# An attention loop over 16 batches on one Trainium2 core: the order of its steps is rewritten over the border between two batches

## The chip, the cores and the metric

The kernel runs on one core of a Trainium2 chip. The metric is device time in microseconds (us) of one execution. Three runs of the kernel before gave 2103.26, 2096.0 and 2092.29 us, median 2096.0. The execution that the profiler recorded took 2089.78 us, with a span of 2088.0 us from its first to its last instruction.

## The reference

The input x has 16 batches of 512 tokens of width 256, all float32. The output is x plus attention plus a mixture of experts, both computed on the layer-normed x:

```python
xn = _layernorm(x)
q, k, v = xn @ Wq.T, xn @ Wk.T, xn @ Wv.T          # 16 heads of 16
q, k = _rope(q, k)
scores = where(causal, -inf, q k^T / 4); attn = softmax(scores) v
logits = xn @ router_w.T + router_bias              # 32 experts, top 4
h = silu(xn @ gate_w.T) * (xn @ up_w.T)             # per expert, width 128
out = sum over the top 4 of score * (h @ down_w.T)  # routed part
out += silu(xn @ sgate_w.T) * (xn @ sup_w.T) @ sdown_w.T   # shared part, width 512
x = x + attn @ Wo.T + out
```

## The kernel before

The kernel has three phases, one after the other, with a barrier between them. Phase A does, batch by batch, the layer norm, the projections, attention, the shared expert and the routing; it scatters the normed tokens into per-expert regions in DRAM (`values`, `table`) and stores x + attention + shared expert (`sum_dram`). Phase B runs 288 blocks of 128 tokens through their experts. Phase D gathers and adds. The change touches phase A alone.

Phase A is written as a list of steps, `ORDER`. Each engine has a handler for the steps in which it takes part, and every engine walks through the same list, so the list is at once the program order of TensorE (PE), VectorE (DVE), ScalarE (ACT), GpSimd (POOL) and of SyncE's DMA queue (SP). Engines meet only by semaphores. An instruction that waits holds up everything behind it on its engine. `FIRST_STEPS` prepares batch 0; then `ORDER` runs for batches 0 to 14, and each body also prepares the next batch (layer norm, q, k, v, routing: the steps in `NEXT_STEPS`); the last batch runs without those and with loads of the expert weights put in (`last_steps`).

The steps, with their lines in the profile of before:

- `("gate", m)`, `("up", m)` (PE L915, two matmuls each), `("gth", m)` (DVE L694) and the product (DVE L702, in the step `up`): the shared expert's hidden layer, m = 0 to 3. The tanh is ACT L570.
- `("s1", g, u)`: six steps for each of four head groups g. PE (L931, L935) computes scores of four heads, DVE (L715) takes the row maxima. `("negsplit", g)` (DVE L726, L727), `("negT", g)` (PE L945, ACT L588) and a small DMA (SP L411) bring the negated maxima into rows of `q_st`.
- `("s2", g, u)`: five steps per group. PE (L962, L973) computes transposed scores less the maxima, ACT (L600) the exponentials. `("av", g, kt)` (PE L990) multiplies with v; `("avT", g)` (DVE L736 to L749) transposes and divides.
- `("down", t)` (PE L1002) and `("oproj", p)` (PE L1011): the shared expert's second matmul and the output projection, summed in one PSUM tile; DVE L757 adds x, SP L417 stores.
- Next batch: `lnA` (DVE L646 to L651, after the load of x by SP L397), `lnB` (L655 to L663), `lnC` (L670); `xT` (PE L880, ACT L526) transposes into `xn_t`; `("qk", j)` (PE L896, DVE L682 to L685 for the rotary embedding, POOL L481, `part0` on ACT L546, POOL L485) makes two-part q and k in `parts`; `("vr", t)` (PE L905, ACT L537, L538) makes v and router logits; `("stack", c)` is 12 SP DMAs (L391) of 128 KB from `parts` to `q_st` and `k_st`, c = 0 for head groups 0 and 1, c = 1 for groups 2 and 3. `route` (DVE L765 to L787), `exps` (ACT L605), `rank` (PE), `rankA`, `rankB`, `rankC` (DVE) pick experts and slots; `copy` (ACT L578) and `("scat", t)` (POOL L494, L496, eight indirect DMAs each) write tokens out.

PSUM buffers set a second order. The steps s1 and s2 share two tiles, `ps_u`, strictly in turn: a step waits until the s1 or s2 step two before it has been read, by DVE for s1 and by ACT for s2. Most other PE steps share three tiles, `ps_g`, in turn. `plans` works out, from the list, whose reader each step waits for.

Of the kernel before, what the change touches and what calls it, by code (L numbers as in the profile page):

```python
# [68 lines left out]
def hold(eng, passed):  # L69
# [9 lines left out]
    ("rankC",), ("gate", 0), ("placeV",), ("s1", 0, 0), ("gth", 0), ("up", 0), ("s1", 0, 1), ("copy",), ("s1", 0, 2),  # L79
    ("gate", 1), ("s1", 0, 3), ("s1", 0, 4), ("gth", 1), ("scat", 0), ("up", 1), ("lnA",), ("gate", 2), ("s1", 0, 5),  # L80
    ("negsplit", 0), ("gth", 2), ("scat", 1), ("s1", 1, 0), ("up", 2), ("s1", 1, 1), ("negT", 0), ("gate", 3),
# [11 lines left out]
    ("exps",), ("stack", 1), ("down", 0), ("down", 1), ("rankA",), ("av", 3, 0), ("av", 3, 1), ("av", 3, 2),  # L93
    ("av", 3, 3), ("avT", 3), ("rankB",), ("down", 2), ("down", 3), ("oproj", 0), ("oproj", 1),
# [3 lines left out]
def attention_steps(with_next):  # L98
    return [s for s in ORDER if with_next or s[0] not in NEXT_STEPS]


def last_steps(order):


    s, piece = [], 0
    for step in order:
        s.append(step)
        if step == ("rankC",):
            s.append(("fill_rows",))
        if step == ("scat", NT - 1):  # L110
            s.append(("fill",))
# [13 lines left out]
     ("stack", 0), ("stack", 1), ("loaded", 1), ("route",), ("exps",),  # L125
     ("rank",), ("rankA",), ("rankB",)]
# [3 lines left out]
            "vr": ("logits",), "tables": ("cos_t", "sin_t"), "rank": ("ranked",)}  # L130
NEXT_STEPS = ("lnA", "lnB", "lnC", "xT", "tables", "qk", "vr", "part0", "stack", "route", "exps", "rank", "rankA",
              "rankB")
# [5 lines left out]
def plans(steps, last_banks, last_units):  # L138


    banks, units, last_banks, last_units = {}, {}, list(last_banks), list(last_units)
    nb = nu = 0
    for step in steps:
        idx, ahead = step[1] if len(step) > 1 else 0, int(step[0] in NEXT_STEPS)
        for k, name in enumerate(BANKS_OF.get(step[0], ())):
            banks[step, k] = (nb, last_banks[nb])
            last_banks[nb] = (name, idx, ahead)
            nb = (nb + 1) % len(last_banks)
        if step[0] in ("s1", "s2") or step == ("down", 0):
# [44 lines left out]
def phase_a(nc, sb_, sem, ident, identb, iota_e, counts, we_gu, we_d, ps_g, ps_u, ps_av, x, wqkvr, wgu_e, wd_e, wo, wgu_s, wd_s, bias,  # L194
            rope_cos, rope_sin, values, sum_dram, table):
    stack = ExitStack()
    with stack:
# [50 lines left out]
        xn_t = in_gu([P, KC, SEQ])  # L248
# [58 lines left out]
        we_in, fill_chain, fill_ready, filled = sem("we_in"), sem("fill_chain"), sem("fill_ready"), sem("filled")  # L307
        neg_parts, tanh_done, av_out, exps, chosen_ready = \
# [14 lines left out]
        body = attention_steps(True)  # L323
        tail = last_steps(attention_steps(False))
# [36 lines left out]
        def _(sp):  # L361
# [32 lines left out]
            def x_load(nb):  # L394
# [19 lines left out]
            def store(b, step, env):  # L414
                if step[1] == 1:
                    sp.wait_ge(S["sums"], 2 * b + 2)
                    sp.dma_start(tokens(sum_dram, b), osum[:, :, :]).then_inc(sum_out, 16)  # L417
# [8 lines left out]
            run(sp, {"loaded": loaded, "stack": stack_rows, "gate": gate, "negT": neg_store, "oproj": store})  # L426
# [92 lines left out]
        def _(act):  # L519
            def xT(nb, step, env):  # L520
                t, bank = step[1], env[0][step, 0][0]
                act.wait_ge(pe["xT"], NT * nb + t + 1)
                if t == 0 and not env[3]:

                    act.wait_ge(pe["up"], NM * nb)
                nc.scalar.activation(xn_t[:, :, t * P:(t + 1) * P],  # L526
# [64 lines left out]
            def s2(b, step, env):  # L591
# [5 lines left out]
                if u == 0:  # L597

                    act.wait_ge(pe["av"], NG * b + (g - 1 if g >= 2 else 0))
# [38 lines left out]
        def _(dve):  # L638
            front = Chain(dve, dve_front, 2 + 3 + 3 * 3 + 6 + 7, passed_dve)
            back = Chain(dve, dve_chain, NG + NG + 4, passed_dve)  # L640
# [78 lines left out]
            def negsplit(b, step, env):  # L719
# [6 lines left out]
                back.link(b, nc.vector.tensor_copy(np_[:, :, 0, :], n_))  # L726
# [3 lines left out]
            def avT(b, step, env):  # L730
# [8 lines left out]
                back.link(b, nc.vector.reciprocal(rden[:], rows[:, :, DH]))  # L739
# [11 lines left out]
            def oproj(b, step, env):  # L751
# [703 lines left out]
```

## Time and profile before

| | before |
|---|---|
| runs, us | 2103.26, 2096.0, 2092.29 |
| profiled execution / its span, us | 2089.78 / 2088.0 |
| PE, DVE busy | 86%, 66% |
| ACT, POOL busy | 36%, 48% |
| phase A ends (last store to `sum_dram` issued) | 1435.9 us after the start |

Busy shares are averages over three unlike phases. PE is TensorE's matmul row; its ends are modelled. A row of the timeline gives start, duration, engine, line, operation, `out<-in`, how many instructions are merged, and in brackets the idle time before and what ended it. In names of tiles `we_gu` and `we_d` stand for buffers of phase A that share the memory of the expert weights (x, xn, xn_t, parts among them).

### The profile page before, as it was taken

How to read it: one execution, taken by the hardware profiler on the slowest of the kernel's cores; microseconds unless marked ns; L12 is line 12 of the kernel's file. 1: busy time of each engine (PE TensorE's matmuls, PEld its weight loads, DVE VectorE, ACT ScalarE, POOL GpSimd, SP SyncE). 2: the span in 40 equal slices, each digit the busy share in tenths (PEclk: the TensorE clock that was granted, in tenths of full speed). 3: DMA queues.
4: the chain of work that ended last, by engine and by line, in shares of the span. 5: the costliest groups of instructions: out<-in, count | busy, mean ns of one | idle time of the engine just before them, and what ended most of it. 6: DMA issues, size and time to landing. Idle time of an engine off the chain costs nothing. (4 is left out here: it accounts for less than half of the span.)

```text
span 2088.0 us, 41196 instructions
## 1 busy us (share of the span) xinstructions
PE 1800.1 (86%) x10415; PEld 1092.9 (52%) x10416; DVE 1377.0 (66%) x3411; ACT 758.2 (36%) x1667; POOL 998.2 (48%) x993
## 2 busy tenths in 40 slices
PE   5898999999999999999999999995999999999300
PEld 2354554545545455454554545543888888888300
DVE  6667668667686675866767667651566666666487
ACT  2334333342343423334234342331444444444200
POOL 5455445553454534545345453473555555555200
PEclk8999999999999999999999999976999999999755
DMA  6251541624506246052460624565555555556499
GB/s 136 78 123 37 108 93 39 127 50 87 111 26 121 54 84 111 27 124 45 90 111 29 121 49 86 104 185 197 150 167 170 168 178 167 172 170 181 136 352 326
DMA packets 217741, 255.29 MB, mean 122 GB/s; under 512 B 74421, under 2 KB 166334, under 8 KB 217536
## 3 DMA queue, kind: packets, MB, share of 16 engines
q1 hardware_dynamic: 160000, 161.90, 33.8%
q0 software_dynamic: 35840, 71.63, 10.7%
q10 hardware_dynamic: 21824, 20.98, 3.1%
q14 instruction: 59, 0.48, 0.1%
q8 instruction: 18, 0.29, 0.1%
HBM read 112.54 MB, written 94.64 MB: 99 GB/s over the span
## 5 line engine op out<-in xcount | busy, mean ns | idle before, releaser
L715 DVE TENSOR_REDUCE neg<-ps_u 128x2 f32<-128x768 f32 (+3 forms) x384 | 391.5, 1044 | 149.7 <-PE ps_u L935 145.4
L494 POOL DMA_INDIRECT table<-entry,slot x256 | 254.4, 994 | 360.6 <-ACT xs L578 260.0
L1204 POOL DMA_INDIRECT y_dram<-yb,ent x288 | 283.4, 984 | 223.5 <-issue 169.7
L496 POOL DMA_INDIRECT values<-xs,slot x256 | 248.6, 971 | 83.3 <-issue 83.3
L915 PE MATMUL ps_g<-we_gu 128*128 128x512 f32 x512 | 243.6, 609 | 0.0
L600 ACT ACTIVATE probs<-ps_u 128x1024 f32<-128x1024 f32 x160 | 159.3, 1021 | 160.0 <-PE ps_u L973 159.6
L600 ACT ACTIVATE we_d<-ps_u 128x1024 f32<-128x1024 f32 x160 | 161.1, 1022 | 152.5 <-PE ps_u L973 152.3
L962 PE MATMUL ps_u<-q_st,k_st 50*128 50x512 f32 (+3 forms) x1024 | 171.6, 394 | 50.7 <-DMA q_st<-neg_t 14.7
L931 PE MATMUL ps_u<-k_st,q_st 48*128 48x128 f32 (+3 forms) x1024 | 185.6, 400 | 31.1 <-DVE neg L715 20.7
L481 POOL TENSOR_TENSOR we_d<-we_d 128x512 f32<-128x512 f32 x64 | 81.3, 1271 | 211.4 <-DVE we_d L685 208.6
L931 PEld LDWEIGHTS ps_u<-k_st,q_st 48*128 48x128 f32 x1024 | 88.2, 189 | 168.2 <-issue 74.2
L1255 PE MATMUL ps_u<-we_d,h_t 128*128 x576 | 173.7, 383 | 0.0
L570 ACT ACTIVATE we_gu<-ps_g 128x512 f32<-128x512 f32 x64 | 38.2, 597 | 349.1 <-PE ps_g L915 349.1
L1336 DVE TENSOR_SCALAR wh<-ent 128x1 f32<-128x1 f32 x288 | 44.3, 154 | 174.2 <-ACT tnh L1151 130.1
L962 PEld LDWEIGHTS ps_u<-q_st,k_st 50*128 50x128 f32 x1024 | 89.0, 201 | 132.6 <-ACT probs L600 38.1
L1241 PE MATMUL ps_g<-we_gu,x_t 128*128 x576 | 150.1, 383 | 3.7 <-issue 3.7
L1241 PE MATMUL ps_av<-we_gu,x_t 128*128 x576 | 149.7, 383 | 1.6 <-issue 1.6
L915 PEld LDWEIGHTS ps_g<-we_gu 128*128 128x128 f32 x512 | 92.8, 194 | 80.0 <-issue 75.5
L1329 DVE COPY x_t<-ps_g 128x256 f32<-128x256 f32 x288 | 120.6, 419 | 12.9 <-PE ps_g L1230 10.9
L1002 PE MATMUL ps_u<-w_d,hid 128*128 128x256 f32 x512 | 125.9, 402 | 0.6
L935 PE MATMUL ps_u<-mask_qk,identb 128*128 128x128 bf16 (+1 forms) x768 | 125.5, 246 | 0.0
L1165 ACT ACTIVATE yb<-ps_u 128x256 f32<-128x256 f32 x288 | 110.6, 384 | 31.2 <-PE ps_u L1255 5.1
(157 smaller groups left out, 3012.7 us busy)
## 6 DMA issues: line engine op xcount, KB each, us to landing
xg<-values SPq DMA_DIRECT2D x288, 128.0 KB
ys<-y_dram SPq DMA_DIRECT2D x64, 512.0 KB, 5.5
q_st<-we_gu SPq DMA_DIRECT2D x192, 128.0 KB, 7.7
k_st<-we_gu SPq DMA_DIRECT2D x192, 128.0 KB, 9.5
we_gu<-x SPq DMA_DIRECT2D x16, 512.0 KB, 6.0
xres<-x SPq DMA_DIRECT2D x16, 512.0 KB, 5.4
sum_dram<-osum SPq DMA_DIRECT2D x16, 512.0 KB, 4.7
we_gu<-wgu_e ACTq DMA_DIRECT2D x16, 512.0 KB, 5.0
```

The source lines that it names most:

```text
L494: pool.indirect_dma_start(table[:, :], bass.IndirectOffsetOnAxis(ap=slot[:, k:k + 1], axis=0), entry[:, k, :], None).then_inc(scattered, 16)
L496: pool.indirect_dma_start(values[:, :], bass.IndirectOffsetOnAxis(ap=slot[:, k:k + 1], axis=0), xs[:, k // TOPK, :], None).then_inc(scatte ...
L600: nc.scalar.activation(probs[g % 2][:, u, :], ps_u[env[1][step][0]][:, :, :].rearrange("p a n -> p (a n)"), ACT.Exp, scale=SCALE).then_inc ...
L715: nc.vector.tensor_reduce(neg[:, g % 2, i, :, k0:k0 + nk], ps[:, :, 0:nk * n].rearrange("p a (k n) -> p a k n", n=n), AX.X, ALU.max, negat ...
L915: ins = nc.tensor.matmul(ps[:, :], w_gu[:, c, lo:lo + P], xn_t[:, c, :], start=(c == 0), stop=(c == KC - 1))
L931: nc.tensor.matmul(ps[:, a, k * n:(k + 1) * n], q_st[rows, h, i * P:(i + 1) * P], k_st[rows, h, 0:n], start=(k == 0), stop=False, skip_gro ...
L935: ins = nc.tensor.matmul(dst, identb[:], mask_qk[:].rearrange("p (o n) -> p o n", o=1).broadcast_to([P, nk, P]), start=False, stop=True, s ...
L962: nc.tensor.matmul(ps[:, a, lo:lo + n], k_st[rows, h, kt * P:(kt + 1) * P], q_st[rows, h, kt * P:SEQ], start=(lo == 0), stop=False, skip_g ...
L1002: nc.tensor.matmul(ps[:, t // 2, (t % 2) * D:(t % 2 + 1) * D], hid[:, m, t * P:(t + 1) * P], w_d[:, m, :], start=(t % 2 == 0 and m == 0), ...
L1204: pool.indirect_dma_start(y_dram[:, :], bass.IndirectOffsetOnAxis(ap=ent[k][:, 0:1], axis=0), yb[k][:, :], None, bounds_check=TOKENS * TOP ...
L1241: ins = nc.tensor.matmul(ps_gu[s][:, 0:2 * HE], x_t[s][:, c * P:(c + 1) * P], w_gu[:, bass.ds(e, 1), c, :], start=(c == 0), stop=(c == KC ...
L1255: nc.tensor.matmul(ps_y[s][:, 0:D], h_t[s][:], w_d[:, bass.ds(e, 1), :], start=True, stop=True).then_inc(y_ps, 1)
```

## The change

The list is written anew, and some steps belong to another batch than the body they stand in. A function `ahead_of` says which: s1, negsplit and negT of group 0 now belong to the next batch (+1) and stand at the end of the body; av and avT of group 3 and the output sum belong to the batch before (-1) and stand at its start. The body has four parts, one for each group; in each, the s1 steps of one group alternate with the s2 steps of the group before it, and av of the group before that stands behind the first s1 step.

```diff
 ORDER = [
+    ("rankC",), ("xload",), ("copy",), ("scat", 0), ("s1", 1, 0),
+    ("av", 3, 0), ("av", 3, 1), ("av", 3, 2), ("av", 3, 3), ("s1", 1, 1), ("avT", 3), ("gate", 0), ("placeV",), ("scat", 1),
+    ("s1", 1, 2), ("gth", 0), ("out", 0, 0), ("s2", 0, 0), ("s1", 1, 3), ("lnA",), ("s2", 0, 1), ("out", 0, 1),
+    ("s1", 1, 4), ("lnB",), ("s2", 0, 2), ("scat", 2), ("out", 1, 0), ("s1", 1, 5), ("s2", 0, 3), ("negsplit", 1),
+    ("lnC",), ("out", 1, 1), ("s2", 0, 4), ("negT", 1), ("store",), ("xres",),
+
+    ("s1", 2, 0), ("av", 0, 0), ("av", 0, 1), ("av", 0, 2), ("av", 0, 3), ("s1", 2, 1), ("avT", 0),
+    ("xT", 0), ("xT", 1), ("xT", 2), ("xT", 3), ("up", 0), ("s1", 2, 2), ("gate", 1), ("s2", 1, 0), ("s1", 2, 3), ("gth", 1),
+    ("s2", 1, 1), ("qk", 0), ("s1", 2, 4), ("s2", 1, 2), ("up", 1), ("s1", 2, 5), ("part0", 0), ("s2", 1, 3),
+    ("negsplit", 2), ("qk", 1), ("s2", 1, 4), ("negT", 2),
+
+    ("s1", 3, 0), ("av", 1, 0), ("av", 1, 1), ("av", 1, 2), ("av", 1, 3), ("s1", 3, 1), ("part0", 1), ("avT", 1),
+    ("stack", 0), ("scat", 3), ("vr", 0), ("s1", 3, 2), ("gate", 2), ("s2", 2, 0), ("s1", 3, 3), ("gth", 2), ("s2", 2, 1),
+    ("up", 2), ("s1", 3, 4), ("s2", 2, 2), ("qk", 2), ("s1", 3, 5), ("s2", 2, 3), ("negsplit", 3), ("vr", 1),
+    ("s2", 2, 4), ("negT", 3), ("part0", 2),
+
+    ("s1", 0, 0), ("av", 2, 0), ("av", 2, 1), ("av", 2, 2), ("av", 2, 3), ("s1", 0, 1), ("vr", 2), ("vr", 3), ("avT", 2),
+    ("s1", 0, 2), ("gate", 3), ("s2", 3, 0), ("s1", 0, 3), ("route",), ("gth", 3), ("s2", 3, 1), ("up", 3), ("s1", 0, 4),
+    ("s2", 3, 2), ("qk", 3), ("s1", 0, 5), ("s2", 3, 3), ("exps",), ("negsplit", 0), ("rank",), ("part0", 3), ("s2", 3, 4),
+    ("rankA",), ("negT", 0), ("rankB",), ("stack", 1),
 ]
+def ahead_of(step):
+    if step[0] in NEXT_STEPS or (step[0] in ("s1", "negsplit", "negT") and step[1] == 0):
+        return 1
+    if step[0] in ("out", "store") or (step[0] in ("av", "avT") and step[1] == NG - 1):
+        return -1
+    return 0
```

`FIRST_STEPS` gets the s1 steps, negsplit and negT of group 0 of batch 0 ahead of `route`. The first body leaves out the steps with -1; a separate `LAST_ORDER` serves the last batch, and an `EPILOGUE` does its av, avT, output sum and store. The loop now takes two batches per turn, since the transposed input has two buffers:

```diff
-        xn_t = in_gu([P, KC, SEQ])
+        xn_ts = [in_gu([P, KC, SEQ]) for _ in range(2)]
...
-            with eng.Fori(1, BATCH - 1) as b:
-                assert (lb, lu) == tuple(map(one_later, steps(body, b, b + 1, False, lb, lu)))
-            steps(tail, BATCH - 1, None, False, lb, lu)
+            with eng.Fori(0, (BATCH - 2) // 2) as i:
+                lb1, lu1 = steps(ORDER, 2 * i + 1, 1, False, lb, lu)
+                assert (lb1, lu1) == (lb, lu), (lb, lb1, lu, lu1)
+                assert (lb, lu) == steps(ORDER, 2 * i + 2, 0, False, lb, lu)
+            lb, lu = steps(tail, BATCH - 1, 1, False, lb, lu)
+            steps(EPILOGUE, BATCH, 0, False, lb, lu)
...
-                    act.wait_ge(pe["up"], NM * nb)
+                    act.wait_ge(pe["up"], NM * (nb - 1))
```

`down` and `oproj` become `out`: for each 128 tokens the four matmuls with `w_d` and the two with `w_o` stand together, in a tile of `ps_g` where they had one of `ps_u`:

```diff
+            def out_part(b, step, env):
+                p_, half = step[1:]
+                t = 2 * p_ + half
+                if half == 0:
+                    bank_of(step, 0, env)
+                ps = ps_g[env[0][("out", p_, 0), 0][0]][:, half * D:(half + 1) * D]
+                if t == 0:
+                    pe_.wait_ge(S["hidden"], done("hidden", b, NM - 1))
+                for m in range(NM):
+                    nc.tensor.matmul(ps, hid[:, m, t * P:(t + 1) * P], w_d[:, m, :], start=(half == 0 and m == 0),
+                                     stop=False, skip_group_check=True)
+                if t == 0:
+                    pe_.wait_ge(S["attn_t"], done("attn_t", b, KC - 1))
+                for c in range(KC):
+                    ins = nc.tensor.matmul(ps, attn_t[:, c, t * P:(t + 1) * P], w_o[:, c, :], start=False,
+                                           stop=(c == KC - 1), skip_group_check=True)
+                if half == 1:
+                    ins.then_inc(pe["sum"], 1)
```

The load of x for the next batch is a step of its own (`xload`), as are `xres` and `store`. In the last batch the loads of the expert weights are issued later, beside s2 of groups 2 and 3 instead of beside nearly all s2 steps:

```diff
-        if step[0] == "s2" and step[1:] != (0, 0) and piece < GU_PIECES:
-            s.append(("load_gu", piece))
-            piece += 1
+        if step[0] == "s2" and step[1] >= 2:
+            n = 2 if piece < 12 else 1
+            s += [("load_gu", piece + k) for k in range(n)]
+            piece += n
```

Two semaphores (`neg_high`, `rden_ready`) replace links of the chain semaphore in negsplit and avT; they order the same instructions.

## Rows read from the trace of the kernel before

**Rows 1.** The page: busy time and share of the span of each engine.

```profile
PE 1800.1 (86%) x10415; PEld 1092.9 (52%) x10416; DVE 1377.0 (66%) x3411; ACT 758.2 (36%) x1667; POOL 998.2 (48%) x993
```

**Rows 2.** Timeline of SyncE's queue: stores of batches 0, 1 and 14, a stack, an x load.

```profile
139.36 0.39 SPq L417 DMA_DIRECT2D sum_dram<-osum  x1
224.67 0.42 SPq L417 DMA_DIRECT2D sum_dram<-osum  x1
632.99 3.80 SPq L391 DMA_DIRECT2D q_st<-we_gu  x6
654.47 0.41 SPq L397 DMA_DIRECT2D we_gu<-x  x1
1347.63 0.42 SPq L417 DMA_DIRECT2D sum_dram<-osum  x1
```

**Rows 3.** Waits of PE, 139.4 to 225 us: total us, times, longest; first of seven.

```profile
PE ps_g L945 <- DVE neg_p L727: 1.1, 1, 1.1
```

**Rows 4.** Timeline of PE in one body.

```profile
578.30 0.50 PE L931 MATMUL ps_u<-k_st,q_st 48*128 48x512 f32 x2
...
578.95 0.44 PE L931 MATMUL ps_u<-k_st,q_st 48*128 48x128 f32 x4
...
585.86 0.50 PE L962 MATMUL ps_u<-q_st,k_st 50*128 50x512 f32 x2
...
587.69 0.51 PE L962 MATMUL ps_u<-q_st,k_st 50*128 50x384 f32 x4 [0.46 <-ACT we_d L600]
...
617.04 2.36 PE L990 MATMUL ps_av<-probs,v_pad 128*32 128x512 f32 x32
...
630.45 0.40 PE L945 MATMUL ps_g<-ident_r,neg_p 128*8 128x128 f32 x4 [1.07 <-DVE neg_p L727]
...
634.26 0.50 PE L962 MATMUL ps_u<-q_st,k_st 50*128 50x512 f32 x2 [1.12 <-DMA q_st<-neg_t]
...
644.89 3.72 PE L1002 MATMUL ps_u<-w_d,hid 128*128 128x256 f32 x16
648.45 3.62 PE L1011 MATMUL ps_u<-w_o,attn_t 128*128 128x256 f32 x16
651.90 1.88 PE L915 MATMUL ps_g<-we_gu 128*128 128x512 f32 x4
```

**Rows 5.** Timeline of DVE: lnA's first, a maximum, a rotary step's last, route's first, avT.

```profile
577.59 1.40 DVE L646 BATCH_NORM_STATS2 stats<-we_gu 128x6 f32<-128x256 f32 x4
...
579.86 1.23 DVE L715 TENSOR_REDUCE neg<-ps_u 128x2 f32<-128x1024 f32 x1
...
596.66 0.69 DVE L685 TENSOR_TENSOR we_d<-ps_g,we_gu 64x512 f32<-64x512 f32 x1
...
630.23 0.29 DVE L765 TENSOR_TENSOR lg<-logits,bias_bc 128x128 f32<-128x128 f32 x1
...
634.61 0.72 DVE L736 STREAM_TRANSPOSE av<-ps_av 128x512 f32<-128x512 f32 x1
```

**Rows 6.** Timeline of POOL: the second POOL instruction behind that rotary step.

```profile
599.75 1.27 POOL L485 TENSOR_TENSOR we_gu<-we_d,we_gu 128x512 fp32r<-128x512 f32 x1 [0.89 <-ACT we_gu L546]
```

**Rows 7.** DMAs issued at 647.5 to 648.6, then 654.3 to 655 us: KB, us to landing.

```profile
k_st<-we_gu SPq DMA_DIRECT2D x2, 128.0 KB, 11.3
...
we_gu<-x SPq DMA_DIRECT2D x1, 512.0 KB, 8.5
```

**Rows 8.** Timeline of DVE, then of PE, in the first body.

```profile
62.59 1.41 DVE L646 BATCH_NORM_STATS2 stats<-we_gu 128x6 f32<-128x256 f32 x4 [8.18 <-DMA we_gu<-x]
...
66.05 0.80 PE L931 MATMUL ps_u<-k_st,q_st 48*128 48x256 f32 x4 [7.88 <-DVE neg L715]
```

**Rows 9.** Stretches: busy us of PE, PEld, DVE, ACT, POOL; clock, DMA share, GB/s.

```profile
61.00:71.00 10.00, 4.95 (x14) 2.65 (x15) 7.85 (x24) 0.59 (x1) 7.76 (x8) 0.52 0.14 45
...
1430.00:1435.00 5.00, 5.00 (x24) 4.21 (x23) 1.04 (x2) 0.00 (x0) 3.42 (x4) 1.00 1.07 388
```

**Rows 10.** Timeline of ACT's queue: the first weight load, in the last batch.

```profile
1368.23 0.46 ACTq L618 DMA_DIRECT2D we_gu<-wgu_e  x1
```

More of the change, by code:

```diff
@@ L78, with last_steps @@
 ORDER = [
[L79 to L81 removed]
[11 rows of a table removed]
[L93 to L102 removed]
+    ("rankC",), ("xload",), ("copy",), ("scat", 0), ("s1", 1, 0),
[3 rows of a table added]
+    ("lnC",), ("out", 1, 1), ("s2", 0, 4), ("negT", 1), ("store",), ("xres",),
[11 rows of a table added]
+    ("rankA",), ("negT", 0), ("rankB",), ("stack", 1),
+]
+LAST_ORDER = [
+    ("rankC",), ("fill_rows",), ("copy",), ("scat", 0), ("scat", 1), ("scat", 2), ("scat", 3), ("fill",), ("s1", 1, 0),
[3 rows of a table added]
+    ("out", 1, 1), ("s2", 0, 4), ("up", 0), ("negT", 1), ("store",), ("xres",),
[6 rows of a table added]
+    ("negsplit", 3), ("s2", 2, 4), ("negT", 3),
+    ("av", 2, 0), ("av", 2, 1), ("av", 2, 2), ("av", 2, 3), ("avT", 2), ("s2", 3, 0), ("s2", 3, 1), ("s2", 3, 2),
+    ("s2", 3, 3), ("s2", 3, 4),
+]
+EPILOGUE = [
+    ("av", 3, 0), ("av", 3, 1), ("av", 3, 2), ("av", 3, 3), ("avT", 3), ("out", 0, 0), ("out", 0, 1), ("out", 1, 0),
+    ("out", 1, 1), ("store",),
+]
+def last_steps():
     s, piece = [], 0
[L106 removed]
+    for step in LAST_ORDER:
         s.append(step)
[L108 to L111, printed above, removed]
[L112 to L114 removed]
+        if step[0] == "s2" and step[1] >= 2:
+            n = 2 if piece < 12 else 1
+            s += [("load_gu", piece + k) for k in range(n)]
+            piece += n
         if step == ("s2", NG - 1, NU2 - 1):
@@ L124 @@
      ("qk", 2), ("vr", 2), ("part0", 2), ("qk", 3), ("vr", 3), ("part0", 3),
-     ("stack", 0), ("stack", 1), ("loaded", 1), ("route",), ("exps",),
-     ("rank",), ("rankA",), ("rankB",)]
+     ("stack", 0), ("stack", 1), ("loaded", 1)] + [("s1", 0, u) for u in range(NU1)] + \
+    [("negsplit", 0), ("negT", 0), ("route",), ("exps",), ("rank",), ("rankA",), ("rankB",)]
 BANKS_OF = {"gate": ("gated",), "up": ("hidden",), "negT": ("neg_t",), "xT": ("xn_t",), "qk": ("rope",),
@@ L424, in loaded @@
                                  ).then_inc(table_set, 16)
-            run(sp, {"loaded": loaded, "stack": stack_rows, "gate": gate, "negT": neg_store, "oproj": store})
+            run(sp, {"loaded": loaded, "stack": stack_rows, "xload": x_load, "xres": xres_load, "negT": neg_store,
+                     "store": store})
             sp.wait_ge(sum_out, 16 * BATCH)
@@ L738, in avT @@
                 rows = av[:].rearrange("p (b c) -> p b c", c=2 * DH)
-                back.link(b, nc.vector.reciprocal(rden[:], rows[:, :, DH]))
+                nc.vector.reciprocal(rden[:], rows[:, :, DH]).then_inc(rden_ready, 1)
+                dve.wait_ge(rden_ready, NG * b + g + 1)
                 if s == 0:
@@ L749, in avT, with out_sum @@
                     nc.vector.transpose(attn_t[:, c, :], attn[:, c, :]).then_inc(S["attn_t"], 1)
-            def oproj(b, step, env):
-                p_, u = step[1], env[1][("down", 0)][0]
+            def out_sum(b, step, env):
+                p_, half = step[1:]
+                if half == 0:
+                    return
+                bank = env[0][("out", p_, 0), 0][0]
                 dve.wait_ge(pe["sum"], 2 * b + p_ + 1)
@@ L851, in _ @@
             run(dve, {"lnA": ln_a, "lnB": ln_b, "lnC": ln_c, "qk": qkv, "gth": gated, "up": hidden, "s1": s1, "negsplit": negsplit,
-                      "avT": avT, "oproj": oproj, "route": route, "rankA": rank_a, "rankB": rank_b, "rankC": rank_c,
+                      "avT": avT, "out": out_sum, "route": route, "rankA": rank_a, "rankB": rank_b, "rankC": rank_c,
                       "fill_rows": fill_rows, "loaded": loaded})
@@ L1038, in _ @@
                       "gate": hidden_part("gate", 0), "up": hidden_part("up", 1), "s1": s1, "negT": negT, "s2": s2, "av": av_,
-                      "down": down, "oproj": oproj, "rank": rank})
+                      "out": out_part, "rank": rank})
 def phase_bcd(nc, sb_, sem, ident, iota_e, counts, we_gu, we_d, ps_g, ps_u, ps_av, values, sum_dram, table, y_dram,
```

92 lines of the change are left out of this document (39 added, 53 removed), and 20 rows, old and new, of tables (LAST_ORDER, ORDER).

## The prediction, written before the changed kernel was run

> **What bounds the kernel now.** I read the page first, then the stores to `sum_dram` as marks of the batches, then the waits of PE, then the timelines of one body. The page has PE busy for 86% of the span and each other engine that computes for two thirds or less [rows 1]. The stores come 224.67 - 139.36 = 85.3 us apart from batch 0 to 1, and (1347.63 - 139.36) / 14 = 86.3 us apart on average [rows 2]. In the 85.3 us body PE waits in seven ways, 5.4 us in all: 1.1 us for the maxima (negT behind negsplit) [rows 3], 1.1 us for their rows (s2 behind the small DMA), and short waits of 0.2 to 0.5 us for a `ps_u` tile [rows 4]. So a body is 79.9 us of PE work. No order of steps changes that work, and 5.4 us a body, some 80 us over 15 bodies, is nearly all that a better order can win.
>
> **The parts of the change.** The same matmuls, maxima and DMAs run in another order, so the sum is one of waits. A, B, C, D are the four parts of the new body, as the list is broken.
>
> *What goes.* Between negT of a group and its first s2 stand six to nine us of PE work in the new list. The way from the one to the other took 634.26 - 630.85 = 3.4 us [rows 4], so that 1.1 us goes, and so does the one at negT where qk, vr or out stands ahead of it. The second `xn_t` lets xT run before the last up; it costs nothing, the ACT copies are the same ones, and no row shows PE waiting for that buffer, so it brings nothing by itself. An `out` step is half of the two down steps' 3.56 us and a quarter of the 3.45 us of both oproj steps, 2.7 us [rows 4], the same work as before. The two new semaphores stand where links of a chain stood: nothing, either way.
>
> *Short waits for `ps_u`.* An s2 that needs the tile of an earlier s2 can start 587.69 - 585.86 = 1.8 us after that one's start: its matmuls, the exponential and two hand-overs [rows 4]. In each part (s2,0), (s1,3), (s2,1) stand in a row, 1.2 us from the first to the third, so 0.6 us is lost; and av waits for the last exponential behind 1.55 us of negT and s1, 0.25 us. Four parts: 3.4 us. Bounds: 0 (the rows of before show 0.46, not always) and 5.
>
> *Part D, route.* route holds DVE for 634.61 - 630.23 = 4.4 us [rows 5]. Before, it stood behind the last maximum of a group. Now it stands between (s1,0,3) and (s1,0,4). After the maximum of (s1,0,3), DVE does route 4.4, gth and hid 0.65 each (like the 0.69 of rows 5, starts overlapping), then the maximum of (s1,0,4), 1.2: 6.9 us. PE is then 1.0 us ahead and has s2 0.65, up 1.8, s1 0.55, s2 0.75, qk 1.8 and 0.6 of short waits to do, 6.2 us [rows 4], before (s1,0,5) needs that tile: 6.9 + 1.0 - 6.2 = 1.7 us of waiting. Next DVE does the rotary step, three instructions of 0.69 [rows 5], and the maximum of (s1,0,5), 1.2: 3.4 us, while PE has s1, s2 and rank, 1.8 us, before (s2,3,4) needs the tile: 1.6 us. Together 3.3. Bounds: 0, since route stood beside PE work without such a wait before, and 5, if DVE comes 1.7 us late to route.
>
> *Part C.* By the same count avT with its second transpose (2.1 us) and the rotary step ahead of (s1,3,5)'s maximum leave PE waiting 0.9 us at (s2,2,4). The stack of groups 0 and 1 is now needed when D starts. It can go once the parts of qk 1 are made, 601.02 - 597.35 = 3.7 us after the rotary step [rows 5, 6], 4.8 us into C. Of such DMAs 24 ran from 632.99 until about 647.8 + 11.3 = 659.1 [rows 2, 7]: 1.0 each and some 2 to start. Twelve are 14.4 us, so the stack is there 19.2 us into C, whose own length I count as 18.9: 0.3 us. Bounds: 0 and 3.
>
> *Part A, the load of x*, the largest term. Stack 1 is the last SP step of a body, and `xload` follows it in the same queue. Before, the stacks were issued from 632.99, 19 us ahead of the body's end. Now stack 1 waits for qk 3, near the end of D, behind route on DVE: its rotary step is done 2.4 us before D ends, and 3.7 us more go through POOL and ACT; and SP first issues the rows of negT 0. Behind negT a stack went out 632.99 - 630.85 = 2.1 us later [rows 2, 4], and ACT now has one exponential to do first. I take 3.0 us into the next body. The stack ends at 3.0 + 14.4 = 17.4. Behind the stack of before, three transfers of 512 KB landed until 654.47 + 8.5 = 663.0, (663.0 - 659.1) / 3 = 1.3 us each [rows 2, 7], so x lands at 18.7. DVE comes to lnA at 11 us and stands there. Behind lnA (2.2 us) come the first output sum (0.7) and the maximum of (s1,1,4) (1.2) [rows 5], done at 22.8. PE comes to (s1,1,5), which needs that tile, after five s1 (3.0; one is 578.95 - 578.30 = 0.65), av 2.3, gate 1.8, three out 8.1, three s2 2.1 and 0.85 of short waits, at 18.1 us [rows 4]. It waits 4.7 us. The first body shows this chain: DVE stood 8.18 us at L646 for x behind a 2 MB DMA, and PE 7.88 us for the maximum behind it [rows 8]. Bounds: 0 if the stack moves fast, 8 if it goes out 3 us later.
>
> One rule of the Trainium skill speaks for a short stack: "DMA: Bandwidth & Descriptors", section "Anatomy of one DMA", fits a transfer as 2.0 us plus its bytes over 436 GB/s. By that, an estimate, 1.57 MB take 5.6 us, x lands near 10 us, before DVE asks, and the term is nothing; the trace, 26.1 us for twice the bytes [rows 2, 7], disagrees and decides.
>
> *A body.* 3.4 + 3.3 + 0.9 + 0.3 + 4.7 = 12.6 us of waits for the 5.4 of before: 85.3 + 7.2 = 92.5 us, against the mean of 86.3: +6.2, and +87 over fourteen bodies. The clock is left as in the 85.3 us body.
>
> *Ends of the phase.* In the first body the table's DMA holds back x, and now also the rows for s2 of group 0. PE went on at 66.05 [rows 8]; now it can at about 61.5, but gates 1 to 3 and ups 0 to 2 (10.8 us) no longer stand ahead of that wait, and 1.3 us of s1 does: 10.8 - 1.3 - 4.5 = +5. In the last batch the loads of the weights, 12.6 MB, began at 1368.23 [rows 10], 21 us after the store of 14 [rows 2]. Now they begin some 38 us before the last store lands. At the 388 GB/s of rows 9 they take 32 us, at the 280 that most slices of that stretch come to, 45: 0 to 7 us stick out; the transpose in the epilogue, no longer covered by down, costs 1.5. Together +6.
>
> **Forecast.** 2089.8 + 87 + 5 + 6 = 2188 us for an execution like the profiled one. The median of the runs shown, 2096.0, is 0.3% above that one; on its scale, 2194 us.
>
> **Rivals.**
> - *x arrives in time.* The stack moves faster when it is alone; the same engines moved 388 GB/s [rows 9], by which it takes 4 us and 2 to start, and x lands near 10. The 4.7 and the 0.3 go: +1.2 us a body, 2089.8 + 17 + 11 = 2118, or 2124 by the median. For it: that rate. Against it: 1.0 us per DMA held to the end of the stacks, when the scatters were over.
> - *Faster: the waits for the maxima go and DVE keeps up.* The place is D and A: DVE reaches route 1.7 us earlier than I count, and x is there. What remains is the 3.4 us for `ps_u`: 83.3 us, 3.0 under the mean, 2089.8 - 42 + 11 = 2059 (2065 by the median). It decides when a body's waits are under the 5.4 us of before. For it: DVE is busy 66% [rows 1]. Against it: rows 8.
> - *Worse: the clock.* Around the 7.88 us wait the granted clock was 0.52 for 10 us [rows 9], half speed, 1.2 GHz. With two such waits a body (A, D), one or two stretches more of a third of that, 1.7 us lost in each, add 24 to 48 us: 2218 to 2242.
> - *No net change.* Gains and waits cancel, 2086 to 2106.
>
> **Chances.** Forecast 0.50, clock 0.16, x in time 0.15, faster 0.13, no change 0.06. A measurement of this kernel can tell about 0.5% from no change. So: faster 0.14, within 0.06, slower 0.80. The range 2105 to 2235 holds the first two and most of the third; the forecast's own is 2160 to 2215.
>
> **What would show it.** In the trace after: stores some 92 us apart; in every body a DVE wait of 5 to 8 us at L646's place for the DMA of x, and behind it a PE wait of 4 to 5 us in s1; a PE wait of 1 to 3 us for the maxima during route; no wait over 0.5 us at negT or for the rows of maxima. The forecast is wrong if x lands before 11 us into the body, or if DVE needs under 5.6 us from route to the next maximum.

## The result, and the profile after

The changed kernel takes 2193.65 us (median of four runs, 2189.65 to 2196.76) against 2097.03 us before: ratio 1.0446, 95% interval 1.0417 to 1.0474, slower by 97 us. The profiled execution took 2189.65 us, its span is 2187.4, 99.4 us over the span before.

The stores of SyncE's queue mark the batches of the changed kernel, as those of [rows 2] do before (start, duration, queue, line):

```profile
168.53 0.41 SPq L453 DMA_DIRECT2D sum_dram<-osum  x1
...
726.13 0.41 SPq L453 DMA_DIRECT2D sum_dram<-osum  x1
820.72 0.41 SPq L453 DMA_DIRECT2D sum_dram<-osum  x1
...
1467.80 0.40 SPq L453 DMA_DIRECT2D sum_dram<-osum  x1
1537.35 0.40 SPq L453 DMA_DIRECT2D sum_dram<-osum  x1
```

Fourteen periods from the first store take 1299.3 us, 92.8 each; before, 1208.3 us, 86.3 each. That is +91.0 us. The first store comes 29.2 us later than before, because more now stands ahead of it, and the last one follows the fifteenth after 69.5 us instead of 88.3: +10.4 for both ends. Phases B and D are 2 us shorter.

The same 14 bodies by what PE waited for (total us, times, longest), in the changed kernel (in the kernel before, the waits of the 14 bodies come to 70.5 us, 5.0 a body):

```profile
PE ps_u L974 <- DVE neg L752: 65.5, 51, 5.5
PE ps_u L1005 <- DVE neg L752: 37.1, 28, 1.6
PE ps_u L974 <- issue: 16.3, 6, 2.8
PE ps_u L1005 <- ACT probs L637: 14.6, 28, 0.5
PE ps_u L1005 <- ACT we_d L637: 8.5, 15, 0.6
PE ps_av L1033 <- ACT we_d L637: 3.7, 20, 0.2
PE ps_av L1033 <- ACT probs L637: 2.5, 14, 0.2
```

L974 is s1, L1005 is s2, and L752 the row maximum. "issue" is time in which PE waited for nothing that the profile shows. With 0.4 us for the stack these are 148.6 us, 10.6 a body. And the busy time of PE, PEld, DVE, ACT and POOL, the clock, the DMA share and GB/s in the same stretch, after and before:

```profile
168.50:1467.80 1299.30, 1146.40 (x6832) 600.38 (x6828) 850.41 (x1774) 457.86 (x700) 576.93 (x559) 0.94 0.37 75
```
```profile
139.40:1347.60 1208.20, 1131.75 (x6834) 599.54 (x6833) 849.79 (x1793) 450.67 (x700) 583.09 (x560) 0.96 0.39 80
```

PE's busy time grew by 14.7 us, at a clock of 0.94 instead of 0.96; the rest of the 91 us, 76.5, is idle time. PE's number of instructions is the same within two and the busy times of the other engines are the same within 8 us: no work was added.

Body 726.1 to 820.7 shows where. First PE, then DVE (in brackets the wait before, and what ended it):

```profile
762.65 0.50 PE L1005 MATMUL ps_u<-q_st,k_st 50*128 50x256 f32 x4 [1.10 <-DVE neg L752]
...
781.02 0.49 PE L974 MATMUL ps_u<-k_st,q_st 48*128 48x512 f32 x2 [1.63 <-DVE neg L752]
784.32 0.63 PE L1005 MATMUL ps_u<-q_st,k_st 50*128 50x256 f32 x4 [1.58 <-DVE neg L752]
...
810.79 0.79 PE L974 MATMUL ps_u<-k_st,q_st 48*128 48x512 f32 x2 [4.38 <-DVE neg L752]
```
```profile
806.57 1.41 DVE L683 BATCH_NORM_STATS2 stats<-we_gu 128x6 f32<-128x256 f32 x4 [7.12 <-DMA we_gu<-x]
```

and SyncE's queue between them, the rows of negT 0, the twelve DMAs of stack 1, the load of x, and that load's time to landing in the last row (KB, us):

```profile
787.04 1.27 SPq L448 DMA_DIRECT2D q_st<-neg_t  x2
788.49 3.80 SPq L431 DMA_DIRECT2D q_st<-we_gu  x6
792.34 3.80 SPq L431 DMA_DIRECT2D k_st<-we_gu  x6
796.43 0.39 SPq L437 DMA_DIRECT2D we_gu<-x  x1
```
```profile
we_gu<-x SPq DMA_DIRECT2D x1, 512.0 KB, 10.0
```

x lands near 806.4, DVE has been standing at lnA for 7.1 us, and PE for 4.4 us behind it. So far the trace is the forecast's.

The next body is another matter. The loop turns in it, near 883 us. PE, then DVE:

```profile
885.23 0.69 PE L974 MATMUL ps_u<-k_st,q_st 48*128 48x128 f32 x4 [2.76 <-issue]
```
```profile
886.57 0.18 DVE L858 TENSOR_TENSOR entry<-pr,zs 128x16 f32<-128x16 f32 x1 [2.85 <-issue]
...
901.25 1.41 DVE L683 BATCH_NORM_STATS2 stats<-we_gu 128x6 f32<-128x256 f32 x4 [2.61 <-DMA we_gu<-x]
```

PE and DVE each stand 2.8 us, one soon after the other, for nothing that the profile shows; ACT has rows until 884.8. DVE then waits only 2.6 us for x, and PE doesn't wait behind it. (The expectations of e2 and e7 below say that all engines stand there; the rows show it for PE and DVE.) The profile page's row of the instruction queue q8 (packets, MB, share of the DMA engines) says what the turn does, before and after:

```profile
q8 instruction: 18, 0.29, 0.1%
```
```profile
q8 instruction: 83, 1.36, 0.3%
```

Before, no packet of q8 falls between 212 and 1348 us: as I read it, the engines held the code of the loop. After, 57 fall between 250 and 1300 us, 16 KB each, with two some 4 us apart at each turn (882.3 and 886.7 here). The 8 KB packets of a second instruction queue, q14, behave alike: none between 209 and 1368 us before, 30 between 250 and 1300 us after. The loop over two batches has twice the code, and it is fetched again on each turn. The prediction had not seen that.

### The profile page after: what moved, and what is told of

The parts are those of the page before. It is cut to its first block and busy times, and to the rows that moved or that the text cites. A ratio compares the mean times of both kernels' runs of the same rounds, so it can differ in the third digit from the quotient of the medians.

```text
span 2187.4 us, 40804 instructions
## 1 busy us (share of the span) xinstructions
PE 1813.2 (83%) x10415; PEld 1092.0 (50%) x10416; DVE 1379.0 (63%) x3411; ACT 766.6 (35%) x1667; POOL 993.0 (45%) x993
## 5 line engine op out<-in xcount | busy, mean ns | idle before, releaser
L752 DVE TENSOR_REDUCE neg<-ps_u 128x2 f32<-128x768 f32 (+3 forms) x384 | 399.9, 1042 | 290.1 <-PE ps_u L978 284.9
L531 POOL DMA_INDIRECT table<-entry,slot x256 | 249.4, 974 | 184.9 <-issue 106.8
L974 PE MATMUL ps_u<-k_st,q_st 48*128 48x128 f32 (+3 forms) x1024 | 190.1, 410 | 105.9 <-DVE neg L752 74.0
L958 PE MATMUL ps_g<-we_gu 128*128 128x512 f32 x512 | 247.2, 605 | 0.0
L637 ACT ACTIVATE probs<-ps_u 128x1024 f32<-128x1024 f32 x160 | 163.9, 1024 | 198.6 <-PE ps_u L1016 196.9
L1005 PE MATMUL ps_u<-q_st,k_st 50*128 50x512 f32 (+3 forms) x1024 | 169.3, 390 | 74.2 <-DVE neg L752 41.8
L974 PEld LDWEIGHTS ps_u<-k_st,q_st 48*128 48x128 f32 x1024 | 91.2, 196 | 259.0 <-issue 124.5
L1005 PEld LDWEIGHTS ps_u<-q_st,k_st 50*128 50x128 f32 x1024 | 86.8, 198 | 168.2 <-DVE neg L752 76.4
L1048 PE MATMUL ps_g<-w_d,hid 128*128 128x256 f32 x512 | 133.0, 406 | 0.0
L938 PE MATMUL ps_g<-we_gu 128*128 128x512 f32 x256 | 121.4, 597 | 0.0
L522 POOL TENSOR_TENSOR we_gu<-we_d,we_gu 128x512 fp32r<-128x512 f32 x64 | 81.4, 1272 | 83.6 <-ACT we_gu L583 83.6
```

The lines of the kernel that those rows point to most:

```text
L531: pool.indirect_dma_start(table[:, :], bass.IndirectOffsetOnAxis(ap=slot[:, k:k + 1], axis=0), entry[:, k, :], None).then_inc(scattered, 16)
L637: nc.scalar.activation(probs[g % 2][:, u, :], ps_u[env[1][step][0]][:, :, :].rearrange("p a n -> p (a n)"), ACT.Exp, scale=SCALE).then_inc ...
L752: nc.vector.tensor_reduce(neg[:, g % 2, i, :, k0:k0 + nk], ps[:, :, 0:nk * n].rearrange("p a (k n) -> p a k n", n=n), AX.X, ALU.max, negat ...
L958: ins = nc.tensor.matmul(ps[:, :], w_gu[:, c, lo:lo + P], xn_ts[env[4]][:, c, :], start=(c == 0), stop=(c == KC - 1))
L974: nc.tensor.matmul(ps[:, a, k * n:(k + 1) * n], q_st[rows, h, i * P:(i + 1) * P], k_st[rows, h, 0:n], start=(k == 0), stop=False, skip_gro ...
L1005: nc.tensor.matmul(ps[:, a, lo:lo + n], k_st[rows, h, kt * P:(kt + 1) * P], q_st[rows, h, kt * P:SEQ], start=(lo == 0), stop=False, skip_g ...
```

## The experiments

Every kernel was run beside the kernel before. One thing has to be known to read them: on each of the three chips of the later runs the kernel before itself took 2579 to 2631 us in place of 2097 (in the profiled run r1, 469 of 498 us of the excess are there when the last store of phase A is issued). The ratios of the first ten kernels hold under that disturbance alone; the last pair removes most of it.

**The load of x alone** (e1, repeated as e5). It is issued from ScalarE's queue, so that it isn't behind the stack:

```diff
-            run(sp, {"loaded": loaded, "stack": stack_rows, "xload": x_load, "xres": xres_load, "negT": neg_store,
+            run(sp, {"loaded": loaded, "stack": stack_rows, "xres": xres_load, "negT": neg_store,
...
-            run(act, {"loaded": loaded, "xT": xT, "tables": tables, ...
+            run(act, {"xload": x_load, "loaded": loaded, "xT": xT, "tables": tables, ...
```

> The changed kernel with one edit: the load of x is issued by ScalarE's queue instead of SyncE's, so it no longer queues behind the 12 DMAs of stack 1. Theory (the load of x behind stack 1 is what holds DVE at lnA and PE behind it): x lands some 5 us after the body starts, the DVE wait for x (7.1 us in one body of two, 2.6 in the other) and the PE wait of 4.4 us behind it go, seven or eight bodies gain 3 to 4.4 us: 2160 to 2170 us. Rival 1 (the shared DMA engines are what x waits for, whatever the queue): x still lands at about 16 us, time unchanged, 2190 us. Rival 2 (DVE is the bound in that part anyway): the wait for x goes, PE waits as long for the maxima, 2185 to 2195 us.

> The changed kernel, with the load of x issued from ScalarE's queue instead of behind the stacks in SyncE's. In the earlier run of this kernel everything in phase A took some 30% longer than in the first measurements (bodies of 115 to 120 us, before and after alike), and the x wait was too small a share to be read. This run repeats it. If bodies are again near 93 us in the changed kernel's way: the DVE waits for x go from 75.5 us in all to under 15 us, the PE waits behind them (4.4 us in each body without a loop turn, seven of them) go, and the loop turn's 2.8 us gap stays: 2193.7 - 31 = some 2163 us, ratio to the kernel before 1.031. Rival: the gap moves to another wait, and the ratio stays at 1.04 to 1.045. If phase A is slow here too (kernel before over 2500 us): ratio 1.018, as it was, with the DVE wait for x near 4 us.

Ratio to the kernel before 1.0178 (1.0133 to 1.0224), then 1.0203 (1.0163 to 1.0243). DVE's waits for x, over the whole execution, in the changed kernel as first measured, in its repetition r2 under the disturbance, and in e1 (4.1 us in e5):

```profile
DVE stats L683 <- DMA we_gu<-x: 75.5, 15, 8.3
```
```profile
DVE stats L683 <- DMA we_gu<-x: 11.1, 3, 4.9
```
```profile
DVE stats L683 <- DMA we_gu<-x: 4.3, 1, 4.3
```

x lands 3.6 us after its issue in e1 and 7.6 us in the changed kernel (medians), so the edit does what it says. It does so by going first: e1 issues x some 2 us ahead of the stack (at 873.32 us, the stack from 875.19), and whether x would be as fast beside the stack isn't shown. But in r2 other stalls had already covered all but 11 us of the wait, and there was next to nothing left to win. What the edit would bring without the disturbance isn't shown.

**Route alone** (e3, repeated as e6): the two last vr steps move from part D to the end of C, and route right behind (s1,0,0).

```diff
-    ("s1", 0, 0), ("av", 2, 0), ..., ("s1", 0, 1), ("vr", 2), ("vr", 3), ("avT", 2),
-    ("s1", 0, 2), ("gate", 3), ("s2", 3, 0), ("s1", 0, 3), ("route",), ("gth", 3), ...
+    ("s1", 0, 0), ("route",), ("av", 2, 0), ..., ("s1", 0, 1), ("avT", 2),
+    ("s1", 0, 2), ("gate", 3), ("s2", 3, 0), ("s1", 0, 3), ("gth", 3), ...
```

> The changed kernel with one edit to the list: vr 2 and vr 3 stand at the end of the third part, and route stands right behind the first score step of the fourth part, where DVE idles 4.2 us, instead of between two maxima. Theory (route in front of a maximum costs PE 3.3 us a body, and delays qk 3, stack 1 and x too): the two PE waits of 1.6 us during the fourth part go or fall under 0.5, stack 1 goes out up to 3 us earlier relative to the rest, 14 bodies gain 3 to 4 us: 2137 to 2155 us. Rival (what is saved in the fourth part comes back as a longer wait for x): 2180 to 2190 us.

> The changed kernel, with route put right behind (s1,0,0) and the last two vr steps ahead of it in the third part. In the changed kernel PE waits 1.6 and 1.6 us around route in each of 15 bodies. My theory: both go, and about 1 us of them comes back elsewhere in the part, since DVE does the same work in it: 15 times 2.2 = 33 us less, 2160 us, ratio 1.030. Rival: DVE's work in the fourth part is simply longer than PE's, so the wait only moves: within 10 us of the changed kernel, ratio 1.04 to 1.045. If phase A is slow here too: ratio 1.02, as it was.

Ratio 1.0200 (1.0156 to 1.0244), then 1.0140 (1.0113 to 1.0166). The second is the lowest of all and lies under e5 and e8, which ran beside it on the same chip (2668 us against 2684 for both); in the first three runs route alone, x alone and both differ by less than their spread. The changed kernel's own interval under the disturbance, below, holds 1.0140, and the changed kernel itself wasn't run in either of these sessions, so a gain isn't shown. The expectation of 1.02 missed by little. Whether the waits of route go or move can't be read from these runs.

**Both, and all repairs** (e4; e8 has in each part the first s2 ahead of the gate or out step as well, so that (s2,0), (s1,3), (s2,1) no longer stand in a row).

```diff
-    ("s1", 0, 2), ("gate", 3), ("s2", 3, 0), ("s1", 0, 3), ("gth", 3), ("s2", 3, 1), ...
+    ("s1", 0, 2), ("s2", 3, 0), ("gate", 3), ("s1", 0, 3), ("gth", 3), ("s2", 3, 1), ...
```

> Both edits, the load of x on ScalarE's queue and route early. Theory (two separate causes): the gains add, 27 plus 45 us: 2115 to 2130 us. Rival (one chain: with x in time route's delay no longer matters, or the other way round): no better than the better of the two by more than 10 us.

> The changed kernel with all repairs: x loaded from ScalarE's queue, route early, and in each part the first s2 ahead of the gate (or output sum) step, so that (s2,g,0), (s1,g+1,3) and (s2,g,1) no longer stand in a row. My theory: of the 10.6 us a body that PE waits, the x wait (2.2 on average), 2.2 of route's 3.2 and some 2.4 of the short waits go, 6.8 us, to 3.8 us a body; the loop turns stay (1.4 a body, in the 10.6). 2193.7 - 15 * 6.8 = 2092 us, ratio 0.998, no better than the kernel before since the loop turn and the ends (10 us) remain. Rival: part of what goes comes back, as DVE has to do the same work: 2130 us, ratio 1.016. If phase A is slow here too: ratio 1.01 to 1.02.

Ratio 1.0180 (1.0136 to 1.0224) and 1.0207 (1.0184 to 1.0231). No repair, nor all together, brought the kernel back to the one before under the disturbance; e8 stayed just above even the 1.01 to 1.02 that I gave it there. What they are worth without it wasn't measured.

**The loop's length alone** (e2, repeated as e7): the kernel before, two batches per turn.

```diff
-            with eng.Fori(1, BATCH - 1) as b:
-                assert (lb, lu) == tuple(map(one_later, steps(body, b, b + 1, False, lb, lu)))
+            with eng.Fori(0, (BATCH - 2) // 2) as i:
+                for k in (1, 2):
+                    assert (lb, lu) == tuple(map(one_later, steps(body, 2 * i + k, 2 * i + k + 1, False, lb, lu)))
```

> The kernel before with one edit: the loop takes two batches per turn, as in the changed kernel, with the order of before. In the changed kernel all engines stand 2.8 us at each turn of the loop and 16 KB fetches on an instruction queue go on through the whole phase, where before they stopped after the second turn. Theory (the doubled loop body is fetched anew in every turn, and this costs 2.8 us per turn by itself): fetches through the phase, six or seven gaps of 2 to 3 us, 2096 + 15 to 20 = 2111 to 2116 us. Rival (the gaps come from the new order, or are hidden when work is queued): no gaps, 2096 us.

> The kernel before, with its loop over two batches per turn instead of one, and no other edit. The changed kernel's trace has all engines idle for 2.8 us at each turn, and some 57 instruction packets in the loop where the kernel before has none. My theory: the doubled body is fetched again at each turn, 7 turns of 2.8 us and little else: 2097 + 20 = 2117 us, ratio 1.009. Rival: fetching also delays other engines in the middle of a body, ratio 1.015 to 1.02 (the earlier run gave 1.016 where phase A was slow). Rival: the loop's length has no price, ratio 1.00.

Ratio 1.0159 (1.0133 to 1.0185), then 1.0169 (1.0146 to 1.0192). The order of the steps is untouched, and the fetches are there, in number the changed kernel's 83; the stores of e7 show the price body by body:

```profile
391.64 0.42 SPq L418 DMA_DIRECT2D sum_dram<-osum  x1
514.99 0.42 SPq L418 DMA_DIRECT2D sum_dram<-osum  x1
631.05 0.41 SPq L418 DMA_DIRECT2D sum_dram<-osum  x1
754.33 0.41 SPq L418 DMA_DIRECT2D sum_dram<-osum  x1
```

123.4, 116.1 and 123.3 us: the first and the third hold a turn and are 7.3 us longer than the second. Over all six turns of e7 the mean difference is 6.1 us (122.0 for 115.9), in e2 it is 6.5. So the loop's length has a price of its own. Under the disturbance it is 43 us in all (46 in e2), as the first rival of e7 had it, and not the 20 us that the gaps alone would make.

**Both kernels again** (r1, r2; two runs of r2), on a second of these chips, without an edit.

> The kernel before, unchanged, to learn whether the chip of the first four experiments, where it took 2616 us instead of 2097, is what slowed everything. Theory (another chip or another placement, on which the supply of instructions is slower): on the chip of the first runs 2090 to 2103 us; on the slow one about 2616 us, with long idle times of the engines that no semaphore explains and fetches of code through the whole phase. Rival (all runs after the first are slow, whatever the chip): 2616 us here too without such fetches.

> The changed kernel, unchanged, beside it. On a chip like the first: 2190 to 2197 us, ratio 1.045. On a chip like that of the four experiments, if the slowness is in the supply of instructions: 2650 to 2700 us, ratio near 1.02, as the four variants had.

Ratio of the kernel before to itself 1.0013 (0.9977 to 1.0050), of the changed one 1.0198 (1.0123 to 1.0273). So the change costs about 2% here and not 4.5%, and the excess isn't any edit's. The supply of instructions, which the expectations suspect, isn't it either: r1 has the 18 packets of q8 of the kernel before, none of them between 261 and 1753 us. The program r1 is the kernel before instruction for instruction; by 76 us it has fallen 1 us behind, and there its first long stall comes. Here POOL, ACT, PE and DVE of r1:

```profile
77.16 0.97 POOL L494 DMA_INDIRECT table<-entry,slot  x1 [0.30 <-issue]
...
78.44 0.97 POOL L496 DMA_INDIRECT values<-xs,slot  x1 [0.30 <-issue]
...
80.98 0.97 POOL L496 DMA_INDIRECT values<-xs,slot  x1 [0.30 <-issue]
81.35 1.02 ACT L600 ACTIVATE we_d<-ps_u 128x1024 f32<-128x1024 f32 x1 [4.52 <-remote]
82.42 0.69 PE L931 MATMUL ps_u<-k_st,q_st 48*128 48x384 f32 x2 [4.22 <-ACT we_d L600]
...
84.18 1.82 DVE L715 TENSOR_REDUCE neg<-ps_u 128x2 f32<-128x768 f32 x2 [8.77 <-PE ps_u L935]
```

and the stretch from 76 to 84 us of r1, then of the kernel before as first measured (columns as above):

```profile
76.00:84.00 8.00, 3.13 (x20) 1.70 (x20) 0.00 (x0) 1.85 (x2) 4.73 (x5) 0.72 0.15 50
```
```profile
76.00:84.00 8.00, 7.82 (x44) 4.54 (x44) 4.53 (x6) 4.10 (x10) 3.89 (x5) 1.00 0.15 49
```

POOL goes on with its indirect DMAs; all others stand, though what they wait for was done (the exponential L600 needs matmuls that ended at 76.8). The DMA engines are no busier than in the kernel before, 0.15. That pointed to the scatters.

**The same pair without the scatters** (n1, n2). In both kernels the indirect DMAs of the steps scat are left out, and phases B to D.

```diff
-                for k in range(TOPK * t, TOPK * (t + 1)):
-                    pool.indirect_dma_start(table[:, :], ...).then_inc(scattered, 16)
-                    pool.indirect_dma_start(values[:, :], ...).then_inc(scattered, 16)
+                pool.tensor_tensor(no_scat[:, :], xs[:, t, 0:1], xs[:, t, 0:1], ALU.add).then_inc(scattered, 1)
```

> The kernel before with two parts left out: the 16 * 32 indirect DMAs of the scatters (one small GpSimd instruction per scat step in their place), and phases B to D (sum_dram is copied to the output at the end, some 45 us). It asks why phase A took 30% longer in the later runs than in the first measurements, and gives a base for its twin. In those runs ACT, DVE, PE and SP stood still for 3 to 7 us at a time while GpSimd's scatters went on. Theory: the stalls hang on the scatters' DMAs. Without them the bodies come back to 85 to 86 us, the last store to some 1436 us, the whole to some 1490 us. Rival: they hang on something else (the small DMAs of the stacks, the rate of instructions): bodies stay at 110 us or more, the whole over 1800 us.

> The changed kernel with the same two parts left out (scatters, phases B to D). If the stalls of the later runs hang on the scatters, this pair shows the change undisturbed. My account of the first measurement: every second body has an x wait (PE some 4.4 us), the others a loop turn (2.8 us), all have route's 1.6 and 1.6, the short waits and the ends, 99 us in all at the end of phase A; none of it needs the scatters: some 1590 us, 90 to 100 us over the twin. Rival: the stack's DMAs move faster with no scatters beside them, x lands before DVE asks at 11 us, and some 30 us go: 60 to 70 us over the twin. If the stalls stay, 30 to 50 us over the twin, as in the full kernels of the later runs.

n1 took 1500.95 us (1495.68 to 1504.97, five runs), n2 1594.03 (1590.59 to 1595.12): 93.1 us more, on a chip where the full kernel before took 2579 us in the same session. Both theories hold: the stalls hang on the scatters' DMAs, and without them the change costs about what it cost in the first measurement. The first and the fourteenth store of n1, and of n2:

```profile
139.87 0.39 SPq L424 DMA_DIRECT2D sum_dram<-osum  x1
...
1265.67 0.41 SPq L424 DMA_DIRECT2D sum_dram<-osum  x1
```
```profile
168.16 0.42 SPq L460 DMA_DIRECT2D sum_dram<-osum  x1
...
1368.76 0.42 SPq L460 DMA_DIRECT2D sum_dram<-osum  x1
```

Thirteen bodies in 1125.8 us, 86.6 each, and in 1200.6 us, 92.4 each: 5.8 us a body for the change, where the first measurement had 6.5. Not all of the 93.1 us is undisturbed: the last batch keeps the indirect DMAs of the fill, and from the fourteenth store to the last n1 is 27.7 us longer than the kernel before as first measured, n2 29.2 longer than the changed one. PE's gap at the loop's turn is in n2 too (16.4 us in six turns) and not in n1. The same waits stand in the same places, here PE in n2's body from 722 to 816 us, and DVE's wait behind which the last of them comes:

```profile
777.08 0.50 PE L979 MATMUL ps_u<-k_st,q_st 48*128 48x512 f32 x2 [1.62 <-DVE neg L757]
780.37 0.63 PE L1010 MATMUL ps_u<-q_st,k_st 50*128 50x256 f32 x4 [1.57 <-DVE neg L757]
805.91 0.79 PE L979 MATMUL ps_u<-k_st,q_st 48*128 48x512 f32 x2 [3.44 <-DVE neg L757]
```
```profile
801.70 1.41 DVE L688 BATCH_NORM_STATS2 stats<-we_gu 128x6 f32<-128x256 f32 x4 [6.20 <-DMA we_gu<-x]
```

And the rival that the stack moves faster without other DMAs beside it holds for a small part alone: x lands 9.1 us after its issue in this body for 10.0 with the scatters, DVE's thirteen waits for it come to 59.2 us (66.1 with the scatters), and PE behind them waits 3.6 us in each second body (4.5 with them). The 30 us of that rival don't go.

## Why the prediction was right, step by step

It said 2194 us and the median is 2193.65; the closeness is partly luck, since errors of both signs cancel. By its steps, over the 14 bodies of the first measurement:

| step | forecast, us a body | measured |
|---|---|---|
| short waits for `ps_u` | 3.4 | 2.9 (30 short ones at s1, 11.4; ACT's four rows, 29.3) |
| part D, route | 1.7 + 1.6 | 1.62 + 1.55 (14 waits each, 22.7 and 21.7) |
| part C, (s2,2,4) | 0.9 | 1.10 (14 waits, 15.4) |
| stack 0 | 0.3 | 0.0 (0.4 in all) |
| part A, x | 4.7 in each | 4.5 in each second one (7 waits, 31.5), so 2.2 |
| loop turn | not seen | 2.7 in six bodies (16.3), so 1.2 |
| sum of the waits | 12.6 | 10.6 |
| body | 92.5 | 92.8 |

*What went* is as said: no PE wait at negT and none for the rows of maxima is among the rows of after, where the kernel before had 1.1 us of each [rows 3, 4].

*Route and part C* came out within 0.2 us (the forecast's 1.6 behind the rotary step is 1.5 by its own terms, 3 x 0.69 + 1.2 - 1.8). They are counts of instructions on DVE between two maxima against PE's work between two uses of one tile, each from the trace of before, and such counts hold when one finds what stands between.

*The load of x* was mechanically right. Forecast: issued behind a stack that goes out 3.0 us into the body and ends at 17.4, landed at 18.7, DVE standing from 11. Measured in body 726: the stack goes out 2.6 us after (s1,1,0) starts at 785.85, from where I count the body; x lands at 20.6; DVE stands from 13.6 (806.57 less 7.12 less 785.85). PE comes to its step at 20.6, where I had 18.1, and goes on at 24.9, where I had 22.8: both are some 2 us late, and so the wait between them, 4.4, came out right. One sum of mine is off: 24 DMAs in 26.1 us with 2 to start make 1.0 each, so twelve are 14.1 us and not 14.4; by that x costs 4.4 and stack 0 nothing, as measured. The failed half is "in every body": where the loop turns, the 2.8 us gap comes before PE's first step of the body while the stack goes out (at 885.03, ahead of (s1,1,0) at 885.23), and the gap takes the place of the wait. Together 3.4 us, not 4.7. I had written of the second `xn_t` that it costs nothing; the doubled loop that it needs has this price.

*The body's base.* I built on the body of 85.3 us and added 7.2. The measured idle time grew by 76.5 / 14 = 5.5 us, and PE's busy time by 1.05 us a body, with the clock at 0.94 for 0.96: from the mean, 86.3 + 5.5 + 1.05 = 92.8. So the waits were overstated by 2 us, and the base understated by 1.0 (85.3 for 86.3) and the clock's 1.05 more. I had the lower clock as a rival with 24 to 48 us in all; it came with 14.7.

*The ends.* Forecast +5 and +6; measured +10.4 to the last store, but not by the parts named. Up to the first store PE is idle 45.4 us for the 36.5 of before. Of these 8.9 us, 3.5 come in the first 70 us, where I had 5; the others lie in the rest of the first body, which has the new waits too (1.62 and 1.57 around route, 2.26 for x) and which my sum over fourteen bodies left out. After the fifteenth store it is 11.5 us for 7.5. PE's busy time at the two ends is 2.7 us less. The weights didn't stick out: they had landed by 1542.2 us, before the last store did, at 1543.3. The price was another, in the last batch: issuing them held ACT.

```profile
1502.86 4.24 ACTq L655 DMA_DIRECT2D we_gu<-wgu_e  x2
...
1507.21 0.59 ACT L625 ACTIVATE neg_t<-ps_g 8x512 fp32r<-8x512 f32 x1 [3.33 <-issue]
```
```profile
1513.65 0.80 PE L1005 MATMUL ps_u<-q_st,k_st 50*128 50x512 f32 x2 [5.29 <-DMA q_st<-neg_t]
```

Two DMA issues took 4.24 us where the other pairs took 0.96 to 1.47; negT's copy stood behind them, and PE for 5.29 us behind its rows, which also shared the DMA engines with the weights (0.98 busy from 1495 to 1525 us). The granted clock was 0.56 in that stretch; over the whole end behind the fifteenth store it was 0.80, before 0.79.

*The rule of the Trainium skill.* "DMA: Bandwidth & Descriptors" of the Trainium skill, section "Anatomy of one DMA", gives its fit for one DMA issued from GpSimd. I had applied it to twelve from SyncE as if they were one transfer, and by that estimate x would have landed near 10 us into the body. The trace has it at 20.6, and at 19.7 in n2, with the scatters gone. What the rival's 388 GB/s had wrong is seen there: while the stack runs, from 787 to 797 us of n2, the DMA engines are full (share 1.08) at 129 GB/s, 1.0 us for each DMA of 128 KB, where in rows 9 a share of 1.07 moved 388 GB/s.

*The other rivals.* "x in time" is refuted by the DVE waits for x in 13 of 14 bodies; "faster" needed waits under 5.4 us a body, and there were 10.6. That the order and not the loop's length is the main cost follows from the rows: in a body without a turn, 726 to 820 us, there is no gap, and its period is 94.6 us; the seven with an x wait take 94.7 us on average, the six with a turn 91.3.

*What stays open.* The share of each wait in the loss is read from PE's idle rows; no run without the stalls takes one of them away. Why the scatters' DMAs stall the other engines on three chips and didn't in the first measurement: the pair n1 and n2 shows that they must be there for it, not what it is. (Phases B to D, which the pair leaves out too, begin behind a barrier after phase A.) Whether the repairs would recover the loss on an undisturbed chip: e1, e3, e4 and e8 ran only under the stalls. And the price of the loop turn alone without them, for which the trace of after gives 16.3 us of PE's time, part of it in place of the x wait.

## What to carry to other kernels

When steps are moved over an iteration's border, write down for each DMA queue what stands in it ahead of the moved load: here 1.5 MB of stacked rows, once issued 19 us before the border, came to stand right ahead of the one load that the next layer norm waits for. Count for each shared tile what the reader's engine must do between two reads against what the writer has to do meanwhile; that gave waits of 1.6 and 1.1 us to within 0.2. And a body doubled for the sake of two buffers can outgrow what the engines hold of its code; look at the instruction queue's packets before and after.

## What the runs showed of the hardware that was not expected

- A loop whose code is held costs no fetches (no packet of q8 within 1136 us), and one of twice the code is fetched anew each turn, in 16 KB packets, with PE and DVE each still for 2.8 us at the turn; under the disturbance of e7 a turn costs 6.1 us.
- Indirect DMAs of 128 rows from GpSimd can hold up the other engines' waits for several microseconds, 27 us a body in r1 and 23 in r2, while the DMA engines are 15% busy in the stretch shown. It was so on three chips and not in the first measurement, with the same program. In n1 only the last batch still has such DMAs (the fill, 32 of them), and only that batch is long, 1467.23 - 1354.45 = 112.8 us where it took 88.3 in the kernel before as first measured.
